# One core of Trainium2, a transformer tower with a slot mixture: a step of three pipelined stages written out in another order, with the slot results turned one step later

## What is computed

```python
def block(x, W, Wq, Wk, Wv, Wo, Wg1, Wg2, slots, scale, fc1, fc2, norm_w):
    h = patches(x) @ W                                  # 64 images, 196 tokens each, 768 -> 192
    q, k, v = silu(h @ Wq), silu(h @ Wk), silu(h @ Wv)  # 12 heads of 16
    energy = einsum('bhnd,bhmd->bhnm', q, k) * decay    # decay = exp(log_slope * (n - m)), n >= m
    out = einsum('bhnm,bhmd->bhnd', energy, v) * sigmoid(h @ Wg1 @ Wg2)
    h = layernorm(h + layernorm(out @ Wo) * ln_w + ln_b)
    xn = rms_norm(h, norm_w)
    logits = einsum('sd,btd->bst', l2(slots) * scale, l2(xn))
    y = einsum('btd,bst->bsd', xn, softmax(logits, axis=-1))   # tokens into slots
    y = einsum('sio,bsi->bso', fc2, gelu(einsum('sio,bsi->bso', fc1, y) + b1)) + b2
    out = einsum('bsd,bst->btd', y, softmax(logits, axis=-2))  # slots back to tokens
    return layernorm(h + out)
```

## Time and profile before

| | |
|---|---|
| median of three runs | 1220.68 us (1220.43 to 1223.71) |
| the profiled execution's own time | 1220.71 us |
| its span | 1219.0 us |
| PE, DVE, ACT, POOL busy | 1105.5, 787.8, 750.0, 595.9 us |
| phase 1, to PE's last instruction of it | 0 to 937.6 us |
| phase 2 | about 938 to 1100 us |
| products, span of PE | 13418 |

### The profile page before, as it was taken

The page is one execution under the profiler, slowest core; times in us unless marked ns, Lnnn a source line. Parts: engine busy times, 40 slices in busy tenths (PEclk is TensorE's granted clock), DMA queues, the critical chain, the costliest instruction groups (busy, mean ns, idle before and its releaser), DMA issues.

```text
span 1219.0 us, 35974 instructions
## 1 busy us (share of the span) xinstructions
PE 1105.5 (91%) x13418; PEld 889.2 (73%) x13418; DVE 787.8 (65%) x2082; ACT 750.0 (62%) x1745; POOL 595.9 (49%) x942
## 2 busy tenths in 40 slices
PE   4899999999999999999999999999998999997563
PEld 3787888888888888888888888788886556564332
DVE  5577766677777777676777777777774222222996
ACT  5567677777777776777777777776763111110676
POOL 3366655565555666555655555665533000000664
PEclk9999999999999999999999999999999999998555
DMA  4411121111111111211111111112063999995786
GB/s 151 197 51 55 58 84 59 62 53 53 53 53 53 53 53 55 80 66 61 55 53 53 53 53 53 53 53 77 32 263 129 368 424 423 424 423 181 235 264 183
DMA packets 50718, 158.41 MB, mean 130 GB/s; under 512 B 5386, under 2 KB 31392, under 8 KB 38372
## 3 DMA queue, kind: packets, MB, share of 16 engines
q1 hardware_dynamic: 33080, 145.09, 32.2%
q10 hardware_dynamic: 17600, 12.78, 3.4%
HBM read 132.23 MB, written 25.62 MB: 129 GB/s over the span
## 4 chain that ended last, share of the span: by engine, by line
PE 71%; DVE 22%; issue 2%; ACT 1%; DVEq 1%; SPq 1%; DMA 1%; POOL 0%; ACTq 0%; POOLq 0%
DVE p_sb L828 9%; PE ps L974 8%; PE ps L976 7%; PE ps L975 7%; PE ps L1271 6%; PE ps L1052 5%; PE ps L1089 4%; PE ps L1290 4%; PE ps L1134 4%; DVE gn L803 3%; PE ps L1031 3%; PE ps L1032 3%; PE ps L1019 2%; PE ps L1157 2%; DVE res L943 2%
## 5 line engine op out<-in xcount | busy, mean ns | idle before, releaser
L427 POOL TENSOR_TENSOR xl<-x_sb,xh 128x392 fp32r<-128x392 f32 x192 | 189.8, 1026 | 84.1 <-DVE gn L803 74.9
L828 DVE TENSOR_TENSOR p_sb<-ps,dec 98x1568 f32<-98x1568 f32 x96 | 171.6, 1788 | 14.8 <-PE ps L1052 14.8
L678 ACT ACTIVATE hg<-ps 128x768 f32<-128x768 f32 x32 | 25.9, 810 | 146.0 <-PE ps L1295 146.0
L768 DVE BATCH_NORM_STATS2 st<-ps 98x6 f32<-98x192 f32 x128 | 40.0, 354 | 77.5 <-PE ps L1019 77.5
L935 DVE COPY y2st<-ps 128x192 f32<-128x192 f32 x32 | 11.4, 358 | 120.5 <-PE ps L1271 120.5
L695 ACT ACTIVATE o_sb<-res,nb,rstd 98x192 f32<-98x192 f32 x128 | 59.5, 535 | 44.8 <-DVE nb L958 44.1
L1089 PE MATMUL ps<-p_sb,vpad 98*32 98x98 f32 x3072 | 84.9, 250 | 1.6 <-DVE p_sb L828 1.6
L1319 PE MATMUL ps<-y2b,cbuf 64*98 64x192 f32 x256 | 49.3, 537 | 38.1 <-POOL y2b L532 38.1
L1089 PEld LDWEIGHTS ps<-p_sb,vpad 98*32 98x32 f32 x3072 | 64.1, 109 | 26.7 <-issue 26.2
L519 POOL CAST pickb<-pick 128x128 fp32r (+1 forms) x32 | 9.4, 293 | 148.8 <-PE ps L1295 148.8
L974 PE MATMUL ps<-xl,wh 128*128 128x392 f32 x192 | 70.1, 365 | 13.1 <-POOL xl L427 13.1
(11 more groups left out here) (203 smaller groups left out, 3484.8 us busy)
## 6 DMA issues: line engine op xcount, KB each, us to landing
x_sb<-in_xT SPq DMA_DIRECT2D x32, 1176.0 KB, 5.2
w1v<-in_fc SPq DMA_DIRECT2D x32, 1152.0 KB, 10.2
w2v<-in_fc SPq DMA_DIRECT2D x32, 1152.0 KB, 12.7
h_dram<-h SPq DMA_DIRECT2D x32, 294.0 KB
h2r<-h_dram SPq DMA_DIRECT2D x32, 294.0 KB
out<-o_sb ACTq DMA_DIRECT2D x32, 294.0 KB
comb_dram<-cst SPq DMA_DIRECT2D x32, 98.0 KB, 1.7
cbuf<-comb_dram SPq DMA_DIRECT2D x32, 98.0 KB, 3.8
```

What stands on the lines that cost most here:

```text
L427: pool.tensor_tensor(xl[:, k], x_sb[:, k], xh[:, k].bitcast(F32), ALU.subtract)\
L828: dve.tensor_tensor(dst, src, rate.unsqueeze(2).to_broadcast([T, 4, 2, TOK]), ALU.mult)\
```

## The change

The same results are computed, with these differences.

- The results of a pair's slots (`combine_turned`, `slot_inputs_turned` and ACT's copies of them) are done in step `i` for pair `i - 3` (new flag `e`), not `i - 2`. The tokens `gn` of a pair are made by DVE one step later than before, in the step that uses them, and `squares` with them.
- `projected(i)` makes keys and queries in one go, keys in banks 2 and 0, queries in 3 and 1: first the products of feature part 0 for all four groups, then those of part 1. The values use banks 4 and 5.
- The second halves of `rows_of_v` and of the projections no longer stand between the scores; `logits`, `combine_turned`, `gate`, `logits_turned` and `slot_inputs_turned` are spread over the places between scores and values.
- The rest `hTl` of part 1 is subtracted by POOL (before: DVE). ACT changes its table between the copy of part 1 and its rounding. The rounding of the next input (`round_x`) and POOL's `split_x` are done in two pieces each, apart.
- `zs` is copied once for 48 partitions, which the weights `wqst` now provide (Wg1 stands in them twice, with zeroed columns between, one load more); the second query group has 112 columns where it had 80.
- `logits_turned` is two transposes of 128 columns, not four products of 64.
- At the start, DVE's work on the output weights and on the slots comes after the first step's scores instead of ahead of the first projections; PE turns the slots (`slots_turned`) at the end of step 0.
- In the last two steps (`last_steps`), ACT does `second_norm` after `tokT` and `squares`, and the pair `i - 3` results are made in step 32.

The diff, cut: first the banks, then SP, POOL, ACT, DVE and PE. Of PE's old `step` only the lines that stay are in it, since its removed lines stand above.

```diff
-V_AT = (2, 7)
+K_AT, Q_AT, V_AT = (2, 0), (3, 1), (4, 5)
...
-            step(0, False)
-            sp.wait_ge(k_mm, 2)
...
+            sp.wait_ge(slT_sb, 1)
...
+            def step(i, a, c, d, e, f, more):
+                if a:
+                    low_h(i, 0)
+                if c:
+                    first_norm(i - 1, 0)
+                if d:
+                    scaled_tokens(i - 2)
+                if a:
+                    low_h(i, 1)
+                if c:
+                    first_norm(i - 1, 1)
                 if d:
                     inverse_norms(i - 2)
...
+                if more:
+                    split_x(i + 1, range(KP // 2))
...
+                if c:
+                    token_scales(i - 1)
                 if more:
-                    if c:
-                        pool.wait_ge(gn_rdy, 4 * i)
...
+                    split_x(i + 1, range(KP // 2, KP))
+                if at_start(i):
+                    slot_norms()
                 if d:
                     combine_weights(i - 2)
...
-                if d:
+                if d and a:
                     second_norm(i - 2)
+                if e and c and not a:
+                    slot_inputs_kept(i - 3, 0, TOK)
+                    combine_kept(i - 3, 0, f)
                 if a:
-                    turned_h(i, 0)
+                    turned_h(i)
+                    if d:
+                        squares(i - 2)
                 if d:
                     act.wait_ge(tokT_mm, i - 1)
                     act.activation(tokT[:, :, :], ps[0:G, 6:8, 0:PT], ACT.Copy).then_inc(tokT_sb, 1)
+                    if c and not a:
+                        squares(i - 2)
+                    if not a:
+                        second_norm(i - 2)
...
+                    act.wait_ge(hT_mm, 2 * i + 2)
+                    act.activation(hT[:, 1], ps[:, 1, 0:PT], ACT.Copy).then_inc(hx_rdy, 1)
                     use_table(ACT.Silu)
-                    turned_h(i, 1)
-                if more:
-                    for k in range(2):
-                        round_x(i + 1, k)
...
+                    act.wait_ge(hx_rdy, i + 1)
+                    act.activation(hTh[:, 1], hT[:, 1], ACT.Copy).then_inc(hTh_rdy, 1)
+                    if more:
+                        round_x(i + 1, 0)
+                    act.wait_ge(k_mm, 2 * i + 1)
+                    act.activation(kA[:, :], ps[:, K_AT[0], 0:PT], ACT.Silu).then_inc(k_sb, 1)
                     act.wait_ge(q_mm, 2 * i + 1)
...
+                    turned_v(i, 0)
                     act.wait_ge(q_mm, 2 * i + 2)
...
+                    act.activation(zs[0:GZ, :], ps[DB:DB + GZ, Q_AT[1], 0:PT], ACT.Copy).then_inc(zh_rdy, 1)
+                    turned_v(i, 1)
+                    act.wait_ge(k_mm, 2 * i + 2)
+                    for a in range(2):
...
+                    last.then_inc(k_sb, 1)
...
+                    if e:
+                        combine_kept(i - 3, 0, f)
+                    if more:
+                        round_x(i + 1, 1)
...
+                elif c:
+                    squares(i - 1)
...
                     use_table(ACT.Exp)
...
+                    slot_exponentials(i - 2)
+                    if not a:
+                        token_exponentials(i - 2)
+                    if a and e:
+                        slot_inputs_kept(i - 3, 1, 0)
+                    dispatch(i - 2)
+                    if a:
+                        token_exponentials(i - 2)
+                    else:
+                        combine_kept(i - 2, 4, e)
+                        slot_inputs_kept(i - 2, 5, 0)
...
+            def step(i, a, c, d, e, f, more):
+                if d:
+                    mean_shifts(i - 2)
                 if c:
...
+                if d and (a or c):
+                    tokens(i - 2)
...
+                if c:
                     residual_statistics(i - 1, 0)
-                if a:
-                    dve.wait_ge(hTh_rdy, 2 * i + 2)
-                    dve.tensor_tensor(hTl[:, 1], hT[:, 1], hTh[:, 1].bitcast(F32), ALU.subtract)\
-                        .then_inc(hTl_rdy[1], 1)
...
-                    cosine_scales(i - 2)
+                    token_norms(i - 2)
...
+                if d:
+                    cosine_scales(i - 2)
                 if a:
+                    dve.wait_ge(zh_rdy, i + 1)
+                    dve.tensor_tensor(zs[ZT:ZK, :], ps[DB:DB + RANK, Q_AT[1], 0:PT], zs[0:RANK, :].bitcast(F32),
...
-                if d:
+                if d and not a:
                     cosines(i - 2)
...
+                if c and not a:
                     tokens(i - 1)
...
                     if d:
+                        cosines(i - 2)
+                    decay(i, 1)
+                    if d:
                         slot_maxima(i - 2)
-                    decay(i, 1)
...
-                if d:
-                    sums(i - 2)
+                    decay(i, 2)
+                if d:
+                    slot_sums(i - 2)
                 if a:
-                    decay(i, 2)
+                    if at_start(i):
+                        output_weights()
                     gated(i, 0)
+                    if d:
+                        shifted_logits(i - 2)
                     gated(i, 1)
...
+                        slot_rows()
+                if d:
+                    token_sums(i - 2)
...
+                for banks, hi, lo, groups, done in (KEYS, QUERIES):
+                    for bank, m in zip(banks, groups):
+                        if bank == Q_AT[1]:
+                            pe.wait_ge(hx_rdy, i + 1)
+                        product(ps[0:m.stop - m.start, bank, 0:PT], hi[:, 0, m], lo[:, 0, m], hTh[:, 0], hTl[:, 0],
+                                True, False)
+                pe.wait_ge(hTl_rdy[1], i + 1)
+                for banks, hi, lo, groups, done in (KEYS, QUERIES):
+                    for bank, m in zip(banks, groups):
+                        product(ps[0:m.stop - m.start, bank, 0:PT], hi[:, 1, m], lo[:, 1, m], hTh[:, 1], hTl[:, 1],
+                                False, True).then_inc(done, 1)
...
-                        mm = pe.matmul(ps[64 * a:64 * a + 64, 0, k * T:(k + 1) * T],
-                                       Lt[0:T, 2 * a + k, :], ident[0:T, 0:T], start=True, stop=True)
+                    mm = pe.transpose(ps[:, 0, k * T:(k + 1) * T], Lt[0:T, 2 * k:2 * k + 2, :], ident[0:T, 0:T])
                 mm.then_inc(lt_mm, 1)
...
+            def full_step(i, c, d, e):
+                embed(i, 0, c, e)
+                if c:
+                    project_out(i - 1, 0)
                 if d:
                     token_features(i - 2)
...
+                embed(i, 1, c, e)
+                if c:
+                    project_out(i - 1, 1)
+                if at_start(i):
+                    pe.wait_ge(loaded, 16 * N_LOADS)
+                    pe.wait_ge(w_split, 12)
+                if c:
+                    pe.wait_ge(t1_rdy, 4 * i - 2)
+                if d:
+                    pe.wait_ge(tokT_sb, i - 1)
+                projected(i)
+                if c:
+                    pe.wait_ge(t1_rdy, 4 * i)
+                rows_of_v(i, 0)
+                rows_of_v(i, 1)
+                h_turned(i, 0)
+                h_turned(i, 1)
+                scores(i, 0, c)
+                pe.wait_ge(hb_sb, i + 1)
+                if d:
                     logits(i - 2)
...
+                keys_turned(i)
+                if e:
+                    combine_turned(i - 3, 0)
+                scores(i, 1, c)
+                if e:
+                    pe.wait_ge(cb_sb, i - 2)
+                gate(i)
+                if d:
+                    pe.wait_ge(Lt_rdy, i - 1)
+                values(i, 0)
+                states(i)
+                if d:
+                    pe.wait_ge(g_sb, 2 * i + 1)
                     logits_turned(i - 2)
...
+                scores(i, 2, c)
+                carried_ready(i)
+                values(i, 1)
+                if e:
+                    pe.wait_ge(g_sb, 2 * i + 2)
+                    slot_inputs_turned(i - 3, 1, 0)
+                carried(i, 0)
+                if d:
                     dispatch_turned(i - 2)
...
+                values(i, 2)
+                if d:
+                    pe.wait_ge(g_sb, 2 * i + 2)
+                    if e:
+                        pe.wait_ge(yT_sb, 2 * i - 4)
                     slot_inputs(i - 2)
...
+                carried(i, 1)
+            def last_steps(i, c):
+                if c:
+                    idle_products(0, 8)
+                    project_out(i - 1, 0)
+                token_features(i - 2)
+                if c:
+                    project_out(i - 1, 1)
+                    combine_turned(i - 3, 0)
+                    slot_inputs_turned(i - 3, 0, TOK)
+                else:
+                    idle_products(1, 6)
+                logits(i - 2)
+                idle_products(1, 12 if c else 2)
+                if c:
```

(32 more changed lines are left out.)

330 lines of the change are left out of this document (128 added, 202 removed).

## The result

The changed kernel is **slower**: median 1260.68 us of four runs (1251.36 to 1270.01) against 1220.85 (1220.43 to 1223.71), ratio 1.032 with a 95% interval of 1.024 to 1.040. The prediction was 1216.5, range 1208 to 1225. Its four runs are 19 us apart, and their mean granted clock falls as they get longer: 0.947, 0.940, 0.939, 0.929. The profiled one is the shortest, 1251.36 with a span of 1249.6, and 30.6 us longer than the span of before.

The account below looks back on a forecast made before the run. The prediction took PE's work plus PE's waits to bound the loop. Loop -13.0, step 2 -1.0, start +1.3 and end +8.5 summed to -4.2 us on 1220.71, giving 1216.5, range 1208 to 1225.

Parts of the forecast that it names:

- The second new wait is on `hb`: Loop, PE after scores 0: `hb` needs `h_turned` whole and ends at 17.6, so PE waits 0.3 a step.
- The wait on `hTl`: Loop, PE between the two projection runs: part 1 arrives at 11.06, PE asks at 10.60, a new wait of 0.46.
- `Lt`, -0.35: Loop, `logits_turned`: two products of 128 columns for four of 64 take half of 0.65, saving 0.35 a step.
- rival 3: Loop: `Lt` saves 0.05, or waits sum 0.15 longer; 0.3 a step or less saved, 1221 us; chance 0.16.
- The wait of 0.10 at scores 2: Loop, PE at scores 2: it arrives at 2.68, decay 1 ends at 2.77, so a wait of 0.1 stays.
- Start: Steps 0 and 1: -1.5 from earlier projections, +2.8 from clock loss after the wait on the slots' turning; together +1.3 us.
- step 2: Step 2 has no pair's results to turn yet, and the shorter `Lt`: -1.0 us.
- step 33: Step 33, with `tokT` ahead of `second_norm` and the shorter `Lt`: -1.1 us.
- The tail: Step 32: later `second_norm` puts `Lt` at 18.0, +6.8; PE waits about 6, half clock afterwards adds +2.8.
- Rival 4: Loop: `hTl` part 1 arrives 0.5 later, PE waits 0.96, a step takes 28.0, the kernel 1231 us; chance 0.11.
- The drain behind a table load: Loop, ACT: a 1.38 us drain makes the `hTl` wait 1.84, the kernel near 1256 us; chance 0.02.

Follow-up runs that it names:

- run 1: Changed kernel with POOL's first three `split_x` pieces back behind the scaling of the queries, with the other three: 1219.93 us, ratio 0.9993.
- run 5: Kernel before the change, with the first three `split_x` pieces moved ahead of the scaling of the queries: 1403.49 us.
- run 7: Changed kernel with `second_norm` of step 32 at its old place, ahead of the slot-input copies, `tokT` and the squares: 1250.45 us.
- run 6: Changed kernel with DVE's residual reading one SBUF tensor instead of two, the addition of `hb` left out: 1268.12 us.
- run 2: Changed kernel with only one of the three early `xl` pieces left at the early place: 1219.26 us.
- run 3: Changed kernel with the three early `xl` pieces computed twice by POOL, a drain between the two rows: 1221.6 us.
- run 8: Changed kernel with the edits of run 1 and run 7 together: 1213.92 us, ratio 0.9942.
- run 9: Run 8 with ACT rounding part 1 of `hT` ahead of its table change: 1197.36 us, ratio 0.9806.
- run 10: Run 9 with `logits_turned` as four products of 64 columns again, at its new place: 1197.89 us.
- run 12: Run 9 with step 0's output weights, slot rows and `slot_norms` earlier, and `combine_turned` between scores 0 and the `hb` wait: 1187.64 us.

## Why the prediction was wrong

- **The step that failed** is "The second new wait is on `hb`": "from about 16.66 to 17.6. Wait 0.3." It let DVE be free when `h_turned` was done, with no term for what stands ahead of `hb` on DVE. The move of half of `split_x` was named in the change and stood in no term of the sum. Measured: residuals 4.06 for 0.75, `hb` ready 18.6 into the step where the sum had 17.6 and run 1 has 17.8, PE stopped for 1.09 between two products (0.27 in run 1). Runs 1 and 5 show the place of the row as the cause, in both kernels.
- **The clock in the loop** had no term. With stops of 0.33 and 1.09 between products in a step the profiled run spent about 17 us at half clock once in the loop (2 x (34.75 x 0.21 + 29.54 x 0.04)); run 7 did so once as well and run 6 four times. The profiles of runs 1, 2, 3, 8 and 9, with stops of 0.33 and less, show none in the loop. That the unprofiled runs of the changed kernel are longer by such losses follows from their clocks alone: 1268.3 us at 0.929 against 1249.6 at 0.947 is 2 x (1268.3 x 0.071 - 1249.6 x 0.053) = 48 us more at half clock, worth up to 24, and the span is 18.7 longer; where in those executions the clock fell is not on record.
- **The wait on `hTl`**, 0.46, was right: the profile has 0.33 from the end of the product ahead, 0.49 from where its successor could have started (429.94 to 430.43). Its cause, the table's load on the path, was right too (run 9).
- **`Lt`, -0.35**, was mis-sized: the form gives 0.06 (run 10), about what rival 3 named (0.05), and the piece with its new place 0.22 (0.65 to 0.43). It was half of a piece whose length I had not looked into. With 0.06 the forecast of a step would have been 27.8 without the block, with 0.22 27.65; run 1 has 27.66. The wait of 0.10 at scores 2 did not come.
- **Start, step 2 and step 33** were right to 0.2. For the start that is partly luck: nine profiles with the same steps 0 and 1 have 58.4 to 60.4 us for them. **The tail** came to 8.7 for 9.6, with its mechanism, `second_norm` behind the copies: `Lt` came 17.6 into the step for 18.0. PE's wait there was 3.79, not 6: PE had already stopped 1.46 for `tokT`, which the forecast did not have, and then ran 24 idle products in 4.52 us where the kernel before, without that stop, had 2.90.
- Rival 4, on the slower side, had the kind of loss right, a longer stop that the step pays in full (0.82 at the stop, 28.48 for 27.66), and the wrong wait: it gave the lateness to `hTl`. Its threshold of 0.5 was not tested. The drain behind a table load did not show: the load took 1.28 (398.87 to 400.16), the dummy began at 400.17, and the wait was 0.49 and not 1.84.

## What to carry to other kernels

When work moves on one engine, look at what runs beside it on the others: POOL's row of three cost nothing beside DVE's decays, and it kept a residual or four numbers of `cosc` busy for 3.3 us. A wait that data will end is cheapest where independent products can stand under it, and a long one can bring the clock down behind it. And an order that loses may hold its gain ready: three moves of a few lines took the changed kernel from 1260.7 to 1197.4, two more to 1187.6.

## What was not expected of the hardware

- Some DVE instructions that read and write only SBUF stop beside POOL's `xl` subtractions, and an unbroken row held them to its end: two residuals 4.06 us beside three, 6.93 beside six, and one of 98x4 3.33 beside three. The trace has them as busy all that time, so that they stand in no list of waits. The Trainium skill (SBUF — State Buffer, Who interferes with whom) tells of the two engines' shared port, with the later one held for the whole instruction; the traces agree in that the residual, its form with one tensor and `cosc` were held and the decay was not, but here they were held for three and six instructions.
- That is not so for every row, nor for every instruction. Beside `xn` (four of 0.53, 412.63 to 414.76 in the earlier trace rows) two residuals took 1.15 in all kernels but run 6's, whose instruction is another, beside one `xl` piece 1.15 too, beside three ahead of a drain 3.05. Inside the row of six, `cmx` took its 0.41, and `Lc`, which begins in the fifth piece, 0.45 in run 1 and 0.62 in run 12, with the last piece at 1.21 for 1.03. What lets DVE in is open.
- The DVE instructions with an operand in PSUM (decay 1.79, `hb` 0.96) were not longer beside POOL in these traces.
